# ScalarE's roundings of expert weights, which release GpSimd's splits, move from the second to the first group of a cycle

## The reference

```python
g = jnp.einsum('bsd,edf->ebsf', h, Wg)            # 8 experts, 256 -> 1024
u = jnp.einsum('bsd,edf->ebsf', h, Wu)
expert_outs = jnp.einsum('ebsf,efd->ebsd', jax.nn.silu(g) * u, Wd)   # 1024 -> 256
expert_output = jnp.einsum('be,ebsd->bsd', gating_probs, expert_outs)
shared = jnp.einsum('bsf,fd->bsd', jax.nn.silu(h @ Sg) * (h @ Su), Sd)
return (1.0 - sg) * expert_output + sg * shared
```

## Time and profile before

| | |
|---|---|
| median of three runs | 2124.18 us (2120.98 to 2127.06) |
| profiled execution | 2124.22 us, of which the span from first to last instruction is 2122.4 us |
| busy share of the span | PE 90%, VectorE 70%, ScalarE 53%, GpSimd 42% |
| first expert stage | up to about 1141 us of the span, nine experts |
| L564 (`split`), one of 288 | median 693 ns, shortest 677, longest 2839 |

### The profile page before, as it was taken

How to read it: one execution, slowest core, us unless ns; L and a number is a source line. 1 busy time by engine, 2 the same in 40 slices (tenths; PEclk the granted TensorE clock), 3 DMA queues, 4 the chain that set the end, 5 groups by cost and what they waited for, 6 DMA issues and landing times. The chain is left out here.

```text
span 2122.4 us, 35240 instructions
## 1 busy us (share of the span) xinstructions
PE 1920.0 (90%) x12206; PEld 1611.6 (76%) x12206; DVE 1482.5 (70%) x2400; ACT 1115.6 (53%) x2117; POOL 899.0 (42%) x858
## 2 busy tenths in 40 slices
PE   5999999999999999999998677999899766959998
PEld 4778878787887878788787555788799645849998
DVE  6777777767777776777776896433588575857776
ACT  4555554545555454555544597232355364636664
POOL 5442251504224150422400085220388234968885
PEclk9999999999999999999999789999999887979999
DMA  4101010010101001010101301310256114556661
GB/s 151 60 1 60 1 59 0 0 59 0 59 0 59 0 0 59 0 59 0 28 1 51 69 3 35 127 42 8 70 193 198 57 27 129 187 184 206 211 214 55
DMA packets 96322, 144.51 MB, mean 68 GB/s; under 512 B 15358, under 2 KB 72608, under 8 KB 96096
## 3 DMA queue, kind: packets, MB, share of 16 engines
q1 hardware_dynamic: 89168, 127.21, 18.6%
q0 software_dynamic: 4928, 12.86, 1.7%
q10 hardware_dynamic: 2128, 3.15, 0.4%
HBM read 111.46 MB, written 14.16 MB: 59 GB/s over the span
## 5 line engine op out<-in xcount | busy, mean ns | idle before, releaser
L314 PE MATMUL ps<-cond_x_lo,cond_w_hi 128*128 128x512 f32 x1008 | 394.5, 391 | 0.0
L406 ACT ACTIVATE cond_h_hi<-cond_h 128x512 fp32r<-128x512 f32 x288 | 177.2, 629 | 267.6 <-DVE cond_h L559 267.6
L564 DVE TENSOR_TENSOR cond_h_lo<-cond_h,cond_h_hi 128x512 fp32r<-128x512 f32 x288 | 261.9, 938 | 4.1 <-ACT cond_h_hi L406 0.3
L330 PE MATMUL ps<-cond_h_hi,cond_d_hi 128*128 128x512 f32 x576 | 228.2, 396 | 24.3 <-DVE cond_h_lo L564 23.6
L660 POOL TENSOR_TENSOR cond_w_lo<-cond_stage_up,cond_w_hi 128x512 fp32r<-128x512 f32 x36 | 57.6, 1599 | 439.2 <-ACT cond_w_hi L406 439.2
L314 PE MATMUL ps<-cond_x_hi_first,cond_w_hi 128*128 128x512 f32 x576 | 226.3, 393 | 9.5 <-POOL cond_w_lo L678 7.9
L314 PE MATMUL ps<-cond_x_hi_first,cond_w_lo 128*128 128x512 f32 x576 | 225.3, 391 | 0.0
L330 PE MATMUL ps<-cond_h_lo,cond_d_hi 128*128 128x512 f32 x576 | 224.5, 390 | 0.0
L450 ACT ACTIVATE cond_h<-ps 128x512 f32<-128x512 f32 x216 | 121.5, 596 | 196.0 <-DVE cond_h_lo L564 152.0
L330 PE MATMUL ps<-cond_h_hi,cond_d_lo 128*128 128x512 f32 x576 | 224.4, 390 | 0.0
L542 DVE TENSOR_TENSOR ps<-cond_p_row,ps 128x512 f32<-128x512 f32 x144 | 99.8, 693 | 176.0 <-PE ps L314 176.0
(11 more groups left out here) (408 smaller groups left out, 5182.5 us busy)
## 6 DMA issues: line engine op xcount, KB each, us to landing
moe_stage_up<-in_L_ffn_expert_wv SPq DMA_DIRECT2D x22, 1024.0 KB, 8.8
typed_stage_up<-in_L_cond_wi SPq DMA_DIRECT2D x11, 1024.0 KB, 5.0
typed_stage_dn<-in_L_cond_wo SPq DMA_DIRECT2D x11, 1024.0 KB, 5.5
moe_stage_dn<-in_L_ffn_expert_proj SPq DMA_DIRECT2D x11, 1024.0 KB, 5.3
cond_stage_up<-in_L_cond_Wg SPq DMA_DIRECT2D x7, 1024.0 KB, 5.1
cond_stage_up<-in_L_cond_Wu SPq DMA_DIRECT2D x7, 1024.0 KB, 7.2
cond_stage_dn<-in_L_cond_Wd SPq DMA_DIRECT2D x7, 1024.0 KB, 9.5
rope_v_now<-rope_v_blk SPq DMA_DIRECT2D x16, 272.0 KB, 2.4
```

The lines of the kernel that those rows point to most:

```text
L314: ins = pe.matmul(bank, ws[:, j, u, w], xs.rearrange("p o n -> p (o n)"), start=(opens and k == 0), stop=(k == 2), skip_group_check=True)
L330: ins = pe.matmul(y_ps[side][d], w[:, 2 * j + r, d * P:(d + 1) * P], xs[:, tile], start=(j == 0 and r == 0 and k == 0), stop=(j == J - 1 a ...
L406: copy = lambda dst, src: act.activation(dst, src, ACT.Copy)
L564: dve.tensor_tensor(h_lo[:, tile], h[:, tile], h_hi[:, tile], ALU.subtract).then_inc(h_ready, 1)
```

## The change

In every cycle ScalarE calls `tasks` right behind the two `round_hidden` of the cycle before, ahead of the wait for `h_ready` and of the first silu, instead of behind `keep(e, c, 1)` of the second group. Nothing else is changed; GpSimd's stream is the same. The condition stands twice because the wait has to follow the tasks.

```diff
                             round_hidden(pe_e, pe_c, 11, 3)
                             round_hidden(pe_e, pe_c, 21, 4)
+                        tasks(e, c, first, last, sums, raws)
+                        if not (first and c == 0):
                             act.wait_ge(h_ready, 4 * g)
                         silu(e, c, p2_done, bank_a, 0)
                         silu(e, c, p3_done, bank_d, 1)
...
                                 round_x(1, T1, 1)
                                 round_x(1, T2, 2)
                                 round_x(1, T4, 1)
-                        tasks(e, c, first, last, sums, raws)
                         if last and c == 4:
                             hyp.round(act)
                         round_hidden(e, c, 12, 1)
```

## The result

The changed kernel takes 2138.46 us (median of four runs, 2137.21 to 2139.93) against 2122.70 us for the kernel before in the same session: ratio 1.0069, 95% interval 1.0057 to 1.0080. It is slower, by 15.8 us in the first comparison and 13.6 in the second; 2136 had been forecast, range 2128 to 2144.

The account below looks back on a forecast made before the run. TensorE's waits for VectorE's splits, disturbed by GpSimd, were taken as the bound. Per change of expert 4 x 1.15 + 0.1 - 3.23 = +1.5 us; eight give +11.8 on 2124.2: 2136 us, range 2128 to 2144.

Parts of the forecast that it names:

- What bounds the kernel: TensorE waits for VectorE's hidden-tile splits, disturbed by GpSimd in cycles with tasks: 3.23 us lost an expert, 123.07 against 119.84.
- the rival that ends on the other side: L678 starts after VectorE's second first-group split and costs nothing there; only c=5 pays: 2099 us, chance 0.14.
- The gain in the second group: With GpSimd's chain moved to the first group, second-group splits run at 0.68 again: 3.23 us gained an expert.
- The order of the two starts: First group: GpSimd's L678 starts at 575.33, 0.09 us ahead of VectorE's second split at 575.42, and blocks it.
- The price of a blocked cycle: c=6, 7, 0 and 1: late second split delays `lower_right` and A22 x T4; 1.15 us each, 4.60 an expert.
- the 0.16 less 0.02: TensorE's restart after a stop costs 0.16 beyond its lateness; 1.17 taken as 1.15, since weight loads may run ahead.
- c=5: Cycle with only raws: L660 goes ahead of the second first-group split; cost 0.1 us, bounds 0 and 0.3.
- The silus: ScalarE's silus wait for the late splits, but TensorE's next group keeps 0.3 us to spare: no second stop.
- rival B: Late silus also hold up TensorE's next group: 0.2 us more in each of 32 cycles, 2142 us, chance 0.12.
- How far the roundings move: ScalarE's roundings in c=5, 6, 7, 0 and 1 run about 8 us earlier, right after the previous cycle's hidden-tile roundings.
- `w_summed`: ScalarE's wait in `tasks` for the weight sums, claimed to be over by then, being from a cycle ago.

Follow-up runs that it names:

- in the second: The unaltered changed kernel measured once more against the kernel before, in five rounds: 2139.29 against 2125.66 us, ratio 1.0063.
- the small copy: Changed kernel plus one useless ScalarE copy of the 128x128 identity in front of the tasks in c=6, 7, 0 and 1: 2099.38 us, ratio 0.9879.
- the experiment behind the wait: Changed kernel with ScalarE's tasks moved behind the wait for h_ready, still in front of the first silu: 2131.98 us, ratio 1.0033 to the kernel before.
- the half with c=0 and 1 alone: Changed kernel with only the tasks of c=0 and 1 moved, those of c=5, 6 and 7 in the old place: 2135.93 us, ratio 1.0050.

## Why the prediction was right

**What bounds the kernel** held. The stops of TensorE were the whole loss: without them an expert takes 119.9 to 120.1 us (119.84 had been worked out), and the kernel 2099 to 2101 (2099 for the rival that ends on the other side).

**The gain in the second group** held: the splits there are free in c=6, 7 and 0 of the changed kernel, and GpSimd ends at 636.20 in the frame of c=6, 1.96 before VectorE's next instruction with two SBUF operands.

**The order of the two starts** held: 0.09 or 0.10 ahead in all 32 cycles where 0.09 had been worked out, and the second split took 2.89 or 2.90 in every one. The prediction gave this step the largest part of its doubt (0.14), and it was the one that decided: shown by the small copy, which turned 0.10 ahead into 0.11 behind and 2138 into 2099. One detail was off. L679 was expected at 2.8 us, itself blocked by the first split; it takes 2.44. It starts 0.18 before the first split ends and loses 0.03 by it.

**The price of a blocked cycle** was a little small: 1.15 forecast, 1.17 to 1.24 measured (16.15 to 16.22 against 14.98), 1.20 in the mean. The second split takes 2.89 and not 2.83 as in the earlier trace rows, and A22 x T4 starts 4.14 behind the first split instead of 3.08, 1.06 late where 1.01 had been worked out. What a cycle loses beyond that lateness is 0.14 in the mean, the 0.16 less 0.02 of the prediction; whether the 0.02 are weight loads that run ahead is not shown. c=5 cost 0.08, forecast 0.1. Four times 0.05 less these 0.02 is, within rounding, what lies between 1.47 and 1.63 an expert, and eight times that the step from 11.8 to 13.0. The medians differ by 13.6 and 15.8; up to 3 us outside the traced execution stay open.

**The silus** were in no stop of the changed kernel, so rival B did not come; the experiment behind the wait showed that it was near. The silus of the changed kernel are 2.2 late, of which 1.3 cost nothing, and TensorE's second group, at 631.58, is 1.2 late by the stop in front of A22 x T4 alone: 0.3 to spare, as forecast.

**How far the roundings move** was misread: in c=6 the sums are rounded 0.62 ahead of the first split instead of 5.81 behind it, 6.4 us earlier and not about 8. No term of the sum uses it.

**`w_summed`** was dismissed in the prediction as a wait that is over, since the sums come from a cycle ago. That is right for the whole change, and only because both places move together: in the half with c=0 and 1 alone this wait was the cost of c=0. The reason given, sums made a cycle ago, rests on the tasks of c=7 having moved as well, which the prediction does not say.

## What to carry to other kernels

When VectorE and GpSimd both read two operands from SBUF, look at the order of their starts and at the length of GpSimd's longest instruction before moving either: a start 0.1 us earlier or later was worth 39 us in 2138 here. Bring the long one behind the last VectorE instruction that others wait for, by exchanging two instructions on the engine that releases it, or cut it into pieces shorter than the slack behind. And when work is moved in front of a wait, fill only the time in which the engine would have stood there, and at most the slack of what waits behind it; the same roundings one line further down cost 1.2 us a cycle.

## What the runs showed of the hardware

Nothing in the mechanism was unexpected; its sharpness was. Starts 0.10 us apart settled 32 times out of 32 who goes first, in both directions, and GpSimd, when it was the first, kept its turn for the whole of 2.4 us. Waiting costs a little less than the time waited, for either engine: a split that waited ended 0.55 us behind the end of GpSimd's instruction, where it takes 0.68 from start to end by itself, and GpSimd's L683 of the small copy, started 0.57 before the second split ended, took 0.44 more than the 2.41 of before. VectorE's L553, with one operand in PSUM, was not held back by L685, which ran at the same time (0.68). And TensorE's clock fell to 0.51 behind a stop of 2.75 us in the first expert and stayed at 1.00 behind one of 1.68 in the same place, which was worth 1.5 us on the next eight matmuls.
